# Second attention of a fused transformer block: maxima in two double PSUM slots, scores in a ring of single banks, exponentials per head

## The chip, the cores and the metric

The program runs on one core of a Trainium2 chip. The metric is the device time of one execution in microseconds; the kernel before took 1678.64 us (median of three runs, 1678.16 to 1680.62). A core has TensorE (matrix products, written PE in the profile, its weight loads PEld), VectorE (DVE), ScalarE (ACT), GpSimd (POOL) and SyncE (SP, which only issues DMAs here). Each has its own instruction stream, and they meet only at semaphores. TensorE writes to PSUM alone: eight banks, each 512 fp32 columns wide over 128 partitions. VectorE and ScalarE read PSUM; GpSimd and DMA don't.

## The reference

The block has three parts, over 4 batches of 1024 tokens of width 128: a first attention (16 heads of 64, causal), a second attention (16 heads whose keys, queries and values have 4 columns), and a mixture of 8 experts. The change lies in the second.

```
Q = (hs @ q_w + q_b).reshape(B, S, H, HD).transpose(0, 2, 1, 3)
K = (hs @ k_w + k_b).reshape(B, S, H, KPH).transpose(0, 2, 1, 3)
V = (hs @ v_w + v_b).reshape(B, S, H, KPH).transpose(0, 2, 1, 3)
scores = jnp.einsum('bhsk,bhtk->bhst', Q[..., :KPH], K) / math.sqrt(KPH)     # KPH = 4, H = 16
attn = jax.nn.softmax(scores, axis=-1)
ao = jnp.einsum('bhst,bhtv->bhsv', attn, V)
...
mla_out = ao @ o_w + o_b
```

## The kernel before, in words

**Groups and items.** The second attention is 16 groups (`N2`), number n = 4·batch + quarter; a group is 4 heads of one batch. A group has 32 items u = 0 to 31. An item's scores are those of two heads: 128 keys against 512 queries each, two matmuls of 32 contraction rows (`scores`, L1857), transposed so that keys lie on the partitions. ScalarE takes their exponentials (`exp`, L2101), and `values` (L1872) multiplies them with the values, two items later, into a PSUM bank `OT`, in four column tiles of the array (eight records an item).

**Maxima.** The exponentials need the row maxima of the scores first. So each item also has a maxima product (`maxima`, L1883): 128 queries against 512 keys for two heads, which VectorE reduces to two columns (`read_item`, L2333). They run 22 items ahead (`LEAD`), hence partly in the next group. After 16 of them the maxima of half a group are found (L1264), split into three bf16 parts by GpSimd (L2204 to L2210), turned by TensorE (`turn_tops`, L1891) and added to the query rows by VectorE (`lower_queries`, L2342), which the scores 0 or 16 of the group wait for. From item 10 of the last group on there are no maxima left; that stretch is the tail.

**PSUM.** Six banks are three double slots, given out in turn to scores and maxima (`slot(n, u, kind)`): scores(u) overwrites the slot of maxima(u-2), and waits for VectorE's read of it (`top_done`); maxima(u) overwrites the slot of scores(u-1), and waits for its exponentials (`e_done`). Bank 6 is `OT`, bank 7 is `SPARE`, which all other products share one after the other (`spare`): turned maxima, turned outputs (L1899), turned attention output (`turn_ao`, L1906), its projection (`project`, L1912), and for the next batch the turned states (L1834), queries and keys (L1840) and values (L1847). The last five come in four pieces, one an item, each between the item's maxima and its values.

**Row groups.** Heads sit on 32-row strips of the array. Scores of item u use strips 0 and 1 or 2 and 3 by u % 2; maxima m use them by m // 2 % 2. So in two items of four they are the same strips.

**Order.** There is no planner: every engine's program is written out, in the order of the functions `group`, and TensorE's order in an item is scores, maxima, spare piece, values of item u-2. Which spare piece comes at which item stands in the constants `TOPS_AT`, `OUTPUTS_AT`, `AO_AT`, `PROJECT_AT`, `HS_AT`, `QK_AT`, `LV_AT`; the items at which ScalarE copies a half of `OT` in `COPIED_AT`. Groups 1, 3 and 7 carry states and half of queries and keys of the next batch, groups 2, 6 and 10 the rest and the values, groups 4, 8 and 12 the attention output of the batch before and half its projection, groups 5, 9 and 13 the other half. Groups 11 and 14 carry none of these and are called plain here.

## Time and profile before

| | |
|---|---|
| runs | 1678.64 us median, 1678.16 to 1680.62 |
| profiled execution, first to last instruction | 1681.5 us |
| PE busy | 1618.6 us (96%) |
| DVE busy | 1440.7 us (86%) |
| ACT busy | 1208.0 us (72%) |
| POOL busy | 460.7 us (27%) |
| largest group on DVE: L2333, reads of maxima, 490 records | 585.4 us |
| largest on ACT: L2101, exponentials, 512 | 524.2 us |
| on PE: L1872 values, L1857 scores, L1883 maxima | 327.8, 198.9, 189.0 us |

The page gives no time of the profiled execution other than its span. The second attention runs from about 790 us to 1471 us of it, with maxima until 1437 us. A duration in a row is the record's own; instructions of one engine overlap at their ends, so what one costs in a stream is the distance between starts. Matmuls are recorded with their way through the array, so two that start together can each show their whole duration, and a busy TensorE need not be the bound: one looks at what each of its instructions was released by.

### The profile page before, as it was taken

Reading aid. Unit: us, or ns where it says so; the run is one execution under the profiler, and the core shown is the slowest. Engines: PE = TensorE matmul, PEld = TensorE weight load, DVE = VectorE, ACT = ScalarE, POOL = GpSimd, SP = SyncE. Lnnn points to the kernel's source line nnn. Section 1 sums busy time; section 2 is a strip of 40 time slices with the busy share of each in tenths; the row PEclk is TensorE's granted clock in tenths of the full one; section 3 lists DMA queues with packets and bytes.
Section 4 is the critical chain, followed back from the end, with each engine's and each line's share of the span. In section 5 each row is a group of like instructions: output and inputs, shape, how many; then the busy total and the mean of one; then the engine's idle time right before and its main releaser. Section 6 shows DMA issues by size and latency. Waiting matters only on the chain.

```text
span 1681.5 us, 38177 instructions
## 1 busy us (share of the span) xinstructions
PE 1618.6 (96%) x14842; PEld 712.2 (42%) x14842; DVE 1440.7 (86%) x2099; ACT 1208.0 (72%) x1208; POOL 460.7 (27%) x563
## 2 busy tenths in 40 slices
PE   7899999999999999998999999999999999989996
PEld 3444444444444444444233333333332332456774
DVE  6877777888888888996999999999999999488888
ACT  5666766666667666654887888788878888775776
POOL 4211112333332323341234232323332332220004
PEclk9999999999999999997999999999999999999998
DMA  5311111011110110011012000200030000000001
GB/s 142 72 39 37 37 37 39 20 37 37 37 37 36 37 37 21 22 32 32 14 39 51 9 12 16 48 12 13 16 74 20 13 16 21 1 8 8 14 13 50
DMA packets 46602, 52.94 MB, mean 31 GB/s; under 512 B 9279, under 2 KB 33551, under 8 KB 46482
## 3 DMA queue, kind: packets, MB, share of 16 engines
q1 hardware_dynamic: 45584, 50.05, 10.2%
q8 instruction: 84, 1.38, 0.3%
q10 hardware_dynamic: 898, 1.22, 0.3%
q14 instruction: 36, 0.29, 0.1%
HBM read 15.07 MB, written 10.49 MB: 15 GB/s over the span
## 4 chain that ended last, share of the span: by engine, by line
PE 85%; DVE 8%; ACT 3%; issue 2%; POOL 1%; ACTq 0%; POOLq 0%; DVEq 0%
PE psum L1872 15%; PE psum L590 15%; PE psum L571 11%; PE psum L1857 9%; PE psum L1883 7%; PE psum L533 5%; PE psum L1503 4%; PE psum L1470 4%; PE psum L608 3%; DVE arena L2333 3%; PE psum L628 2%; PE psum L553 1%; ACT arena L2101 1%; PE psum L554 1%; PE psum L555 1%
## 5 line engine op out<-in xcount | busy, mean ns | idle before, releaser
L2333 DVE TENSOR_REDUCE arena<-psum 128x2 f32<-128x1024 f32 x490 | 585.4, 1219 | 39.2 <-PE psum L1883 33.0
L2101 ACT ACTIVATE arena<-psum 128x1024 f32<-128x1024 f32 x512 | 524.2, 1026 | 131.6 <-PE psum L1857 117.9
L755 ACT ACTIVATE arena<-psum 128x2048 f32<-128x2048 f32 (+1 forms) x160 | 274.0, 1713 | 229.0 <-PE psum L571 228.9
L1872 PE MATMUL psum<-arena 128*32 128x256 f32 x4096 | 327.8, 392 | 0.7
L859 POOL TENSOR_SCALAR_AFFINE_SELECT arena<-arena 128x512 f32<-128x512 f32 (+1 forms) x160 | 152.5, 971 | 508.9 <-ACT arena L755 508.9
L590 PE MATMUL psum<-arena,hs 128*64 128x512 f32 (+3 forms) x1536 | 283.0, 496 | 0.2 <-POOL arena L859 0.2
L571 PE MATMUL psum<-arena 64*128 64x512 f16 (+3 forms) x2304 | 215.0, 324 | 2.1 <-DVE arena L907 1.6
L1857 PE MATMUL psum<-arena 32*128 32x512 bf16 x1024 | 198.9, 385 | 3.7 <-DVE arena L2333 3.0
L1883 PE MATMUL psum<-arena 32*128 32x512 bf16 x980 | 189.0, 382 | 6.0 <-ACT arena L2101 2.4
L907 DVE TENSOR_TENSOR arena<-arena 128x1024 f16<-128x1024 f32 x64 | 78.4, 1226 | 101.5 <-ACT arena L734 101.5
L590 PEld LDWEIGHTS psum<-arena,hs 128*64 128x64 f32 x1536 | 96.0, 136 | 141.5 <-issue 125.2
L571 PEld LDWEIGHTS psum<-arena 64*128 64x128 f16 x2304 | 96.5, 94 | 132.8 <-issue 57.1
L1857 PEld LDWEIGHTS psum<-arena 32*128 32x128 bf16 x1024 | 48.1, 91 | 215.5 <-issue 145.6
L1872 PEld LDWEIGHTS psum<-arena 128*32 128x32 f32 x4096 | 81.6, 108 | 112.1 <-issue 95.1
L1576 ACT ACTIVATE arena<-psum,b1T 128x1024 f16<-128x1024 f32 x64 | 71.3, 1115 | 51.0 <-PE psum L1470 48.3
L2204 POOL CAST arena<-arena 128x16 bf16<-128x16 f32 x32 | 8.2, 255 | 345.2 <-DVE arena L1264 345.2
L2251 POOL TENSOR_TENSOR arena<-arena,minus_one 128x16 f32<-128x16 f32 x30 | 87.2, 2906 | 53.9 <-ACT arena L2121 53.6
L1503 PE MATMUL psum<-arena 128*128 128x128 f16 x1536 | 92.6, 221 | 7.2 <-issue 5.4
L1503 PEld LDWEIGHTS psum<-arena 128*128 128x128 f16 x1536 | 89.5, 99 | 16.0 <-issue 8.7
L533 PE MATMUL psum<-arena 128*128 128x512 f16 x384 | 93.8, 381 | 0.7 <-ACT hs L740 0.4
L1349 DVE TENSOR_TENSOR arena<-arena 128x1024 f16<-128x1024 f32 x59 | 71.7, 1222 | 22.4 <-ACT arena L1577 22.2
L1470 PE MATMUL psum<-arena 128*128 128x512 f16 x384 | 88.6, 379 | 1.7 <-ACT arena L1577 1.7
(221 smaller groups left out, 2127.5 us busy)
## 6 DMA issues: line engine op xcount, KB each, us to landing
arena<-arena SPq DMA_DIRECT2D x30, 512.0 KB, 2.9
arena<-arena SPq DMA_DIRECT2D x46, 128.0 KB, 2.2
arena<-latent_q SPq DMA_DIRECT2D x64, 64.0 KB, 2.0
arena<-latent_k SPq DMA_DIRECT2D x64, 64.0 KB, 2.0
arena<-arena SPq DMA_DIRECT2D x60, 64.0 KB, 2.3
X<-in_L_attn_states SPq DMA_DIRECT2D x4, 512.0 KB, 4.6
latent_q<-arena SPq DMA_DIRECT2D x16, 96.0 KB, 2.2
latent_k<-arena SPq DMA_DIRECT2D x16, 96.0 KB, 2.3
```

The costliest lines, as they stand in the source:

```text
L533: last = nc.tensor.matmul(dst[:, half * HALF:(half + 1) * HALF], w_now[:, 2 * j + w, :], x_now[:, x, half * HALF:(half + 1) * HALF], start ...
L571: last = nc.tensor.matmul(SC[:, s, c:c + w], k[rows, kt * P:(kt + 1) * P], q[rows, q0:q0 + w], start=(m == 0), stop=(m == 2), skip_group_c ...
L590: last = nc.tensor.matmul(OUT[s * DH:(s + 1) * DH, q0:q0 + w], vals[par][:, kt, s * DH:(s + 1) * DH], probs[g][:, s, c:c + w], start=first ...
L755: nc.scalar.activation(probs[g], SC[:, :, 0:WIDTH[g]], ACT.Exp, scale=DH ** -0.5).then_inc(exp_done, 1)
L859: return nc.gpsimd.affine_select(out=v, in_=v, compare_op=ALU.is_ge, fill=0.0, base=0, pattern=[[0, blocks], [1, P]], channel_multiplier=-1)
L1470: last = nc.tensor.matmul(HP[c][:, half * HALF:(half + 1) * HALF], w1_e[par][:, w, c * P:(c + 1) * P], mT[:, x, tok], start=(m == 0), stop ...
L1503: last = nc.tensor.matmul(YP[slot][:, tok], h[slot][c][:, tok], w2_e[par][:, w, c, :], start=(c == 0 and m == 0), stop=(c == FC - 1 and m ...
L1857: last = nc.tensor.matmul(dst[:, i * HALF:(i + 1) * HALF], k_rows[par][rows, kt * P:(kt + 1) * P], q_rows[par][rows, h * HALF:(h + 1) * HA ...
L1872: last = nc.tensor.matmul(OT[ROWS * c:ROWS * (c + 1), h * HALF // 2:(h + 1) * HALF // 2], v_cols[par][:, kt, 2 * pr + i, :], e_probs[u % 4 ...
L1883: last = nc.tensor.matmul(dst[:, i * HALF:(i + 1) * HALF], q_rows[par][rows, qt * P:(qt + 1) * P], k_rows[par][rows, kh * HALF:(kh + 1) * ...
L2101: nc.scalar.activation(e_probs[u % 4], src, ACT.Exp, scale=KD ** -0.5).then_inc(e_done, 1)
L2333: nc.vector.tensor_reduce(half_tops[:, kh, qt, 2 * pr:2 * pr + 2], src.rearrange("p (i c) -> p i c", i=2), AX.X, ALU.max).then_inc(top_don ...
```

## The change

- `MAXIMA` holds two double slots (banks 0 to 3) for maxima alone: maxima(u) waits only for VectorE's read of item u-2 (`maxima_free`). In TensorE's order they now come ahead of the item's scores.
- `RING` holds three single banks (4, 5, 6). Each head's scores take one (`half_scores`), each has its own semaphore count and its own exponential over 512 columns (`half_exp`, 2 an item), and waits for the exponential three uses back (`ring_free`).
- All other products take one more bank of that ring in turn (`spares`, `ring(n, u, 2)`), each as a whole in one item: four tiles at once rather than one an item. They wait for the exponential of the item before, and the second scores item behind them waits until they were taken (`spare_taken`). Queries and keys are one matmul of 512 columns a half; values of the next batch come in two halves with a read on VectorE each. `OT` moves to bank 7.
- `maximum(n, m)` reorders maxima inside a quarter, so that their strips are always those that the item's scores don't use.
- The constants move by up to two items; the last group's tail uses the maxima slots as a double slot for scores, and exponentials of full width, as before.

`order` shows the streams as they are issued: engine instruction, tile, and the semaphores it waits for. On TensorE in group 4 around item 15, before (L1857 scores, L1883 maxima, L1872 values, L1912 projection):

```order
L1857 MATMUL psum<-arena 128x512 [waits top_done]
L1857 MATMUL psum<-arena 128x512
L1883 MATMUL psum<-arena 128x512 [waits e_done]
L1883 MATMUL psum<-arena 128x512
L1912 MATMUL psum<-arena 128x128
L1872 MATMUL psum<-arena 32x256 [waits e_done]
L1872 MATMUL psum<-arena 32x256 x3
L1857 MATMUL psum<-arena 128x512 [waits top_done,tops_ready]
L1857 MATMUL psum<-arena 128x512
L1883 MATMUL psum<-arena 128x512 [waits e_done]
L1883 MATMUL psum<-arena 128x512
L1912 MATMUL psum<-arena 128x128
```

The same place of the changed kernel (L1902 scores of a head, L1927 maxima, L1916 values, L1957 projection):

```order
L1927 MATMUL psum<-arena 128x512 [waits top_done]
L1927 MATMUL psum<-arena 128x512
L1902 MATMUL psum<-arena 128x512 [waits e_done,tops_ready]
L1902 MATMUL psum<-arena 128x512 [waits e_done]
L1957 MATMUL psum<-arena 128x128 [waits ow_in,ao_ready,e_done]
L1957 MATMUL psum<-arena 128x128 x3
L1916 MATMUL psum<-arena 32x256 [waits e_done]
L1916 MATMUL psum<-arena 32x256 x3
L1927 MATMUL psum<-arena 128x512 [waits top_done]
L1927 MATMUL psum<-arena 128x512
L1902 MATMUL psum<-arena 128x512 [waits e_done] x2
L1916 MATMUL psum<-arena 32x256 [waits e_done]
```

The maxima stand first and no longer wait for `e_done`; the two scores wait singly; the projection's four tiles stand together where one stood in each of four items, behind a wait for `e_done`.

On ScalarE around the copy of half of `OT`, before (L2101 exponential, L2115 copy, L2121 copy of turned outputs):

```order
L2101 ACTIVATE arena<-psum 128x1024 [waits ov_done,sc_done] x13
L2115 COPY arena<-psum 128x256 [waits out_turned,ov_done]
L2101 ACTIVATE arena<-psum 128x1024 [waits ov_done,sc_done] x3
L2121 COPY arena<-psum 128x256 [waits out_scaled,out_turned]
L2101 ACTIVATE arena<-psum 128x1024 [waits ov_done,sc_done] x5
```

and in the changed kernel (L2164 exponential of a head, L2184, L2190 the same copies):

```order
L2164 ACTIVATE arena<-psum 128x512 [waits sc_done]
L2164 ACTIVATE arena<-psum 128x512 [waits sc_done,ov_done]
L2184 COPY arena<-psum 128x256 [waits out_turned,ov_done]
L2164 ACTIVATE arena<-psum 128x512 [waits sc_done]
L2164 ACTIVATE arena<-psum 128x512 [waits sc_done,ov_done]
L2164 ACTIVATE arena<-psum 128x512 [waits sc_done]
L2164 ACTIVATE arena<-psum 128x512 [waits sc_done,ov_done]
L2164 ACTIVATE arena<-psum 128x512 [waits sc_done]
L2164 ACTIVATE arena<-psum 128x512 [waits sc_done,ov_done]
L2164 ACTIVATE arena<-psum 128x512 [waits sc_done]
L2190 COPY arena<-psum 128x256 [waits out_scaled,out_turned]
L2164 ACTIVATE arena<-psum 128x512 [waits sc_done,ov_done]
```

Each exponential is now two, and the copy stands between the two halves of an item.

The diff, cut to its core:

```diff
-        SLOT = [bank(0, 2), bank(2, 2), bank(4, 2)]
+        MAXIMA = [bank(0, 2), bank(2, 2)]
+        RING = [bank(4), bank(5), bank(6)]
-        OT, SPARE = bank(6), bank(7)
+        OT, SPARE = bank(7), bank(6)
-        TOPS_AT, OUTPUTS_AT = (28, 12), (20, 4)
+        TOPS_AT, OUTPUTS_AT = (29, 13), (20, 4)
-        AO_AT, PROJECT_AT, LAST_PROJECT_AT = (6, 22), 14, 27
-        HS_AT, QK_AT, LV_AT = (6, 14), (22, 6), 14
+        AO_AT, PROJECT_AT, LAST_AO_AT, LAST_PROJECT_AT = (8, 24), 16, 22, 27
+        HS_AT, QK_AT, LV_AT = (8, 16), (24, 8), (11, 16)
+        def ring(n, u, use):
+            others = sum(len(s) for s in SPARES[:n]) + sum(x < u for x in SPARES[n])
+            return RING[(2 * (ITEMS * n + u) + use + others) % 3]
+        def maximum(n, m):
+            if n == 0 and m < LEAD + 2:
+                return m // 4, m // 2 % 2, m % 2
+            return m // 4, 1 - m % 2, m // 2 % 2
...
+            def queries_keys(b, h, dst):
+                pe.wait_ge(hsT_ready, 2 * b + h + 1)
+                nc.tensor.matmul(dst, w_lat[:, :], hsT[:, h * HALF:(h + 1) * HALF], start=True, stop=True).then_inc(qk_ps, 1)
...
+            def spare(n, u):
+                kind, k, h = SPARES[n][u]
+                dst = ring(n, u, 2)
+                upto(pe, e_done, 2 * (ITEMS * n + u))
...
+            def ring_free(n, u, i):
+                at = 2 * (ITEMS * n + u)
+                if i == 0 and u - 2 in SPARES[n]:
+                    spare_taken(*SPARES[n][u - 2])
+                elif i == 0:
+                    upto(pe, e_done, at - 1 if u - 1 in SPARES[n] else at - 2)
+                else:
+                    upto(pe, e_done, at if u - 1 in SPARES[n] else at - 1)
...
                 for u in range(ITEMS):
+                    if not in_tail(n, u):
...
+                        maxima_free(n, u)
+                        maxima(n + g, (par + g) % 2, m, MAXIMA[u % 2])
                     if u % 16 == 0:
                         pe.wait_ge(tops_ready, 2 * n + u // 16 + 1)
-                        pe.wait_ge(top_done, tops_by(n + g, m))
-                    scores(par, u, slot(n, u, 0))
-                    g, m = divmod(LEAD + u, ITEMS)
-                        upto(pe, e_done, ITEMS * n + u)
-                        maxima(n + g, (par + g) % 2, m, slot(n, u, 1))
-                    spare(b, gi, u, last)
+                    if in_tail(n, u):
+                        tail_scores(n, par, u)
+                    else:
+                        for i in range(2):
+                            ring_free(n, u, i)
+                            half_scores(par, u, i, ring(n, u, i)).then_inc(sc_done, 1)
+                    if u in SPARES[n]:
+                        spare(n, u)
...
+            def half_exp(n, u, i):
+                if i == 0:
+                    upto(act, ov_done, ITEMS * n + u - 3)
+                act.wait_ge(sc_done, 2 * (ITEMS * n + u) + i + 1)
+                nc.scalar.activation(e_probs[u % 4][:, i * HALF:(i + 1) * HALF], ring(n, u, i), ACT.Exp, scale=KD ** -0.5
+                                     ).then_inc(e_done, 1)
```

## Rows read from the trace of the kernel before

**Rows 1.** Groups on VectorE, second attention while maxima run (us, mean ns | idle before).
```profile
L2333 DVE TENSOR_REDUCE arena<-psum 128x2 f32<-128x1024 f32 x490 | 585.4, 1219 | 39.2 <-PE psum L1883 33.0
```

**Rows 2.** Who waited for whom in the same stretch (us in total, times, longest).
```profile
PEld psum L1883 <- ACT arena L2101: 65.8, 221, 1.5
...
DVE arena L2333 <- PE psum L1883: 33.0, 115, 2.0
```

**Rows 3.** Timeline of all engines, quiet items (start us, us, engine).
```profile
1351.30 0.39 PE L1883 MATMUL psum<-arena 32*128 32x512 bf16 x2
...
1351.62 0.64 PE L1872 MATMUL psum<-arena 128*32 128x256 f32 x8
...
1352.19 0.39 PE L1857 MATMUL psum<-arena 32*128 32x512 bf16 x2
...
1352.41 0.39 PE L1883 MATMUL psum<-arena 32*128 32x512 bf16 x2
1352.62 2.13 ACT L2101 ACTIVATE arena<-psum 128x1024 f32<-128x1024 f32 x2 [0.27 <-PE psum L1857]
...
1353.70 0.39 PE L1883 MATMUL psum<-arena 32*128 32x512 bf16 x2
```

**Rows 4.** Timeline, VectorE: the lowering before group 0 and before group 15.
```profile
790.29 0.42 DVE L2342 TENSOR_TENSOR arena<-psum,arena 128x512 bf16<-128x512 bf16 x1 [1.77 <-PE psum L1891]
...
1423.02 0.41 DVE L2342 TENSOR_TENSOR arena<-psum,arena 128x512 bf16<-128x512 bf16 x1
```

**Rows 5.** Groups on VectorE in the plain group 11, 1259.2 to 1299.1.
```profile
L2333 DVE TENSOR_REDUCE arena<-psum 128x2 f32<-128x1024 f32 x33 | 39.1, 1220 | 1.4 <-PE psum L1883 1.1
```

**Rows 6.** Timeline, VectorE: reads with work waiting, after a lowering and a projection.
```profile
1194.70 0.41 DVE L2342 TENSOR_TENSOR arena<-psum,arena 128x512 bf16<-128x512 bf16 x1
1195.03 1.21 DVE L2333 TENSOR_REDUCE arena<-psum 128x2 f32<-128x1024 f32 x1
...
1202.28 0.68 DVE L2360 TENSOR_TENSOR acc<-psum,acc 128x512 f32<-128x512 f32 x1
1202.87 8.30 DVE L2333 TENSOR_REDUCE arena<-psum 128x2 f32<-128x1024 f32 x7
```

**Rows 7.** Timeline, TensorE: an item with a turned tile, one with a projected tile.
```profile
1100.31 0.39 PE L1857 MATMUL psum<-arena 32*128 32x512 bf16 x2
1100.31 0.39 PE L1883 MATMUL psum<-arena 32*128 32x512 bf16 x2
1100.63 0.33 PE L1834 MATMUL psum<-ident,hs 128*128 128x128 f32 x1
1100.89 0.64 PE L1872 MATMUL psum<-arena 128*32 128x256 f32 x8
...
1195.17 0.48 PE L1912 MATMUL psum<-arena 64*128 64x128 f32 x2 [0.36 <-DVE arena L2342]
1195.58 0.64 PE L1872 MATMUL psum<-arena 128*32 128x256 f32 x8
```

**Rows 8.** Timeline, ScalarE: instructions that follow each other without a wait.
```profile
847.88 0.58 ACT L2089 COPY arena<-psum 128x512 f32<-128x512 f32 x1
848.34 2.13 ACT L2101 ACTIVATE arena<-psum 128x1024 f32<-128x1024 f32 x2
...
1219.63 1.02 ACT L2101 ACTIVATE arena<-psum 128x1024 f32<-128x1024 f32 x1 [0.27 <-PE psum L1857]
1220.55 0.37 ACT L2115 COPY arena<-psum 128x256 f32<-128x256 f32 x1
```

**Rows 9.** Groups on ScalarE: the dearest half-width form.
```profile
L2095 ACT ACTIVATE arena<-psum,b_lat 128x512 f32<-128x512 f32 x6 | 4.1, 682 | 0.0
```

**Rows 10.** Windows: busy us of each engine, then the granted clock.
```profile
795.00:800.00 5.00, 4.94 (x43) 1.22 (x44) 4.74 (x9) 3.28 (x4) 0.00 (x0) 0.66 0.00 2
```

**Rows 11.** Timeline, TensorE: items at the lower clock.
```profile
796.15 0.61 PE L1857 MATMUL psum<-arena 32*128 32x512 bf16 x2
...
797.71 0.60 PE L1857 MATMUL psum<-arena 32*128 32x512 bf16 x2
```

More of the change, by code:

```diff
@@ L1848, in latent_values @@
+            def latent_values(b, h, dst):
+                pe.wait_ge(hsT_ready, 2 * b + 2)
+                for t in range(GH):
+                    at = (GH * h + t) * P
+                    last = nc.tensor.matmul(dst[:, t * LAT:(t + 1) * LAT], hsT[:, at:at + P],
                                             w_lv[:, :], start=True, stop=True, skip_group_check=True)
-                if two == GH - 1:
-                    last.then_inc(lv_ps, 1)
-            def scores(par, u, dst):
+                last.then_inc(lv_ps, 1)
@@ L1997, in turn_half @@
             def turn_half(k, h, two):
[L1999 to L2001 removed]
+                if two == 0 and k > 0:
                     pe.wait_ge(lg_ready, 2 * (k - 1) + h + 1)
```

378 lines of the change are left out of this document (196 added, 182 removed).

## Prediction, made before the changed kernel ran

> **What bounds the kernel now.** I first read the groups of instructions by line for the stretch in which maxima run (790 to 1437 us), engine by engine. TensorE is busy nearly all of it, but its records overlap, so that says little. VectorE's reads of the maxima are 490 of 1.219 us, 585 us in all, and the idle time before them is 39.2 us, nearly all put down to the maxima product [rows 1]. VectorE is therefore close to its own bound, and 39.2 us is what the trace shows it losing. The waits say why: the maxima product waited 221 times for an exponential, 65.8 us, and VectorE then waited 115 times for the maxima, 33.0 us [rows 2]. The three double slots tie the two together: maxima(u) must wait until the exponentials of item u-1 have left their slot.
>
> The timeline of two quiet items shows this loop [rows 3]. Maxima start at 1351.30, values 0.32 later, scores 0.57 after these (1352.19), maxima 0.22 after the scores (1352.41), and the next maxima at 1353.70: 2.40 us for two items. TensorE's own part of an item is thus 0.57 + 0.22 + 0.32 = 1.11 us. The rest is the wait for ScalarE: the exponential that starts at 1352.62 with 1.02 us ends at 1353.64, and the maxima go at 1353.70, 0.06 later. What VectorE needs is less: with work waiting, seven reads take 8.30 us, so (8.30 - 1.22)/6 = 1.18 us from start to start; a lowering of queries costs it 0.33 (1194.70 to 1195.03) and the addition of a projected half 0.59 (1202.28 to 1202.87) [rows 6].
>
> Fifteen groups run from the lowering at 790.29 to that at 1423.02, 632.7 us [rows 4], 42.2 a group and 1.318 an item. The plain group 11 takes 39.9 us and has only 1.4 us of idle before its reads [rows 5], so 38.5 us of it is VectorE's work (32 reads of 1.18 are 37.8, two lowerings 0.7). The gap between 39.9 and 42.2 is made in groups that carry spare pieces: each piece stands between maxima and values, and the loop through the exponentials has no room for it. One turned tile puts 0.26 us ahead of the values (1100.63 to 1100.89), one projected tile 0.41 (1195.17 to 1195.58) [rows 7].
>
> **The change, part by part.** *Maxima in their own double slot.* The wait for the exponential goes. What is late next is VectorE itself: maxima(u) is released when the read of u-2 ends. From there 0.06 to the start (as after the exponential above), 0.39 through the array, 0.04 to the read: ready 0.49 us after release, wanted 1.18 after. TensorE may be 0.69 us late without any loss.
>
> *Opposite strips.* Where maxima and scores sit on different strips, both start at 1100.31 and the next instruction comes at 1100.63 [rows 7]: 0.32 for both, against 0.22 + 0.32 on the same strips. All items but the first few now have this, so TensorE's item falls from 1.11 (or 0.90 in the half that had it) to 0.90 us. It waits 0.28 us of each 1.18 and has that to catch up with.
>
> *Exponentials per head.* ScalarE's 512-column copy costs 0.46 from start to start (847.88 to 848.34), the 1024-column exponential 0.92 (1219.63 to 1220.55) [rows 8]. Two halves are then 0.92 to 1.0; the dearest half-width form is recorded at 0.682 [rows 9]. A price below 0.46 is excluded by the columns (half of 0.92). I take 0.50 a half: 1.00 an item, 0.18 below VectorE's 1.18, and the four copies of a group fit in that. Both halves lie beside VectorE's reads and cost nothing; if that cover goes, each 0.01 us of a half above 0.57 costs 0.02 an item, some 10 us in all.
>
> *The new waits.* The second score waits for the first exponential of the item before. Scores are ready 0.49 us after their item's release, so by the prices above that exponential ends at 0.99, ahead of the next release at 1.18: no wait. A spare product waits for the second exponential of the item before, which ends at 1.49, 0.31 us into its own. Queued behind it are the values and the next maxima. With 0.4 as start, a product of X us, 0.57 of values and the 0.43 from maxima to read, VectorE goes idle only if 0.4 + X + 0.57 + 0.43 exceeds 2 x 1.18 = 2.36, that is X above 0.96 us. Turned maxima and outputs (four a group, 60 in all) are well below. Of the whole pieces that stood in four items (30: six halves each of states, queries and keys, values, attention output, projection) four turned tiles cost at most 4 x 0.26 = 1.04, four others at most 4 x 0.41 = 1.64. Upper bound: 12 x 0.08 for turns, 6 x 0.68 for queries and keys, 6 x 0.09 for projections (VectorE's own 0.59 covers the rest), none for values, 5.6 us in all; lower bound zero, since a product in one piece pays its way in and out of the array once. I take 3.
>
> The Trainium skill, TensorEngine Tiling (Array Packing), section Key Properties, says that changing the tiling mode drains the engine. By that rule most of the 0.26 of one turned tile is the switch and a fourth tile costs little, so the 3 would be nearer 0; by the row alone, times four, the turns keep their 1.04.
>
> *VectorE's other work.* Values of the next batch in two reads instead of one, three times: at most one more fixed part each, 0.5 in all. Lowerings are unchanged. The lowering for items 16 and 0 comes one item later and is done about 2.8 us after the release of item 13 or 29, with items 16 and 32 released at 3.9: no wait. SyncE's loads move only with the group's pace.
>
> *The first group.* Its start stays: the longest single wait for maxima, 2.0 us [rows 2]. Ten small ScalarE instructions stand between its exponentials; two halves and one of them are at most 1.46 us against 1.18, so 0 to 2.8, taken as 1.4. Everything else, jitter and the passage into the tail, I put at 1. The tail itself has no maxima, keeps its full exponentials and its double slot: 0, within 1 us either way.
>
> **Sum.** What stays of the idle time is 2.0 + 1.4 + 3 + 0.5 + 1 = 7.9 us. From the recorded idle: 39.2 - 7.9 = 31.3 us saved. The record leaves out gaps that are too short to count, so I also go by pace: 632.7 - 15 x 38.5 - 6 x 0.59 = 51.7 us, less three reads of values (2) and 52 small statistics instructions of groups 0 to 3, whose place in the stream no row gives (at 0.1 each, 5), is 44.7; less the lowering's own wait at 790.29, 1.8 [rows 4], and 7.9, 35.0 us. I take 34, nearer the second, since it includes what the first leaves out. The profiled span is 1681.5 us, 0.2% above the median of the runs, and the page shows nothing around it; a saving of 34 us is the same against either. 1678.6 - 34 = 1644.6 us.
>
> **Rivals.** *A: the whole pieces starve VectorE.* For: they stand in one block and wait for an exponential first. Against: the 0.28 us an item to catch up. If each of the 30 costs 0.4 us more than I took, 12 us are lost: 1657 us.
>
> *B: ScalarE sets the pace; the other side.* Place: two exponentials an item. If a half costs h from start to start, an item costs 2h plus 0.03 for the copies; the kernel is slower from 2h + 0.03 = 1.318, h = 0.645. The form at 0.682 [rows 9] would make 1.39 an item, 480 x 0.075 = 36 us lost against before: 1715 us. At 0.60, 1.23 an item, it is just under the forecast's mean item (1.318 - 34/480 = 1.247) and only leaves no room behind long pieces, about 1650. Against: the two distances of rows 8, both well below their records.
>
> *C: the lower clock; also slower.* The granted clock is 0.66 on average in 795 to 800 us, at the stage's start, behind TensorE's waits there [rows 10], and an item then takes 1.56 us (796.15 to 797.71) [rows 11], VectorE waiting. 0.66 is a mean of the two levels, 2.4 and 1.2 GHz. The changed kernel has TensorE wait in every item. It is slower from 34/(1.56 - 1.18) = 90 items at the low level; 160 make 61 us lost, 1705 us. Against: the same products in a shorter time, waits of 0.3 us at most. The Trainium skill speaks for it: TensorE: Matmul & The Clock Gate, section A second HAM failure mode: psum-queue depth-cycling, says that cycling through PSUM banks lets TensorE idle briefly so often that its clock swings. Before the change it already cycled through three slots, at full clock outside the start.
>
> *D: the change doesn't do what it says:* reads are 1.18 apart only in short runs, and 1.20 is the real pace. Then 480 x 0.02 = 10 us less: 1655.
>
> **Chances.** Forecast 0.62, with its own range 1635 to 1652; A 0.14; D 0.10; B 0.05, of which 0.03 slower and 0.02 no change; C 0.05; something unforeseen in the waits 0.04, of which 0.03 slower. The range takes in A, D and B at 0.60: 1634 (nearly all of the 44.7 gone) to 1666. A change of 0.2%, 3.4 us, is about what a measurement of this kernel can tell from none. Faster: 0.62 + 0.14 + 0.10 = 0.86; the same 0.02 + 0.01 = 0.03; slower 0.03 + 0.05 + 0.03 = 0.11.
>
> **What would show it.** VectorE's idle before reads below 10 us, with no wait of the maxima product for ScalarE; reads 1.18 apart in quiet items; a plain group of 38.5 to 39 us and the other groups from 4 on within 1.5 us of it; exponentials of 512 columns recorded near 0.59 with under 1.1 us for a pair from start to start; the clock at 1.00 through the stage. It would be wrong if exponential pairs fill ScalarE, if TensorE's waits name the exponentials ahead of scores in quiet items, or if the items behind a whole piece run well over 1.18 us.

## The result, and the profile after

The changed kernel takes 1631.11 us (median of 4 runs, 1628.53 to 1633.24) against 1678.46 (4 runs, 1678.16 to 1680.62) for the kernel before on the same chip: a ratio of 0.9703, 95% interval 0.9685 to 0.9722. The forecast of 1644.6 had the direction and what the change frees, but the gain is 47 us, not 34, and 1631.1 lies 3 us below its range: the forecast priced VectorE's read of the maxima at 1.18 us where it costs 1.131.

The profiled executions differ by 50.1 us (1681.5 against 1631.4). VectorE's lowerings ahead of group 0 and of group 15 say where:

```profile
786.19 0.42 DVE L2417 TENSOR_TENSOR arena<-psum,arena 128x512 bf16<-128x512 bf16 x1 [0.49 <-PE psum L1936]
...
1370.44 0.41 DVE L2417 TENSOR_TENSOR arena<-psum,arena 128x512 bf16<-128x512 bf16 x1
```

The fifteen groups take 584.3 us, against 632.7 [rows 4]: 48.5 saved. The 4.1 us ahead of group 0 and the 2.6 lost behind group 15 (258.4 us to the end before, 261.0 now) go with the clock, as shown below.

The groups on VectorE and ScalarE over the whole program (busy us, mean ns | idle before):

```profile
L2408 DVE TENSOR_REDUCE arena<-psum 128x2 f32<-128x1024 f32 x490 | 565.7, 1214 | 11.1 <-PE psum L1927 9.8
L2164 ACT ACTIVATE arena<-psum 128x512 f32<-128x512 f32 x980 | 519.6, 600 | 52.0 <-PE psum L1902 46.1
```

The idle time before the reads fell from 39.2 [rows 1] to 11.1. That is 28 us of 48.5: the rest is in the busy time, which fell by 20 although nothing about the read changed. A group's busy time counts records that overlap once, so reads that follow each other closely look cheaper. The waits, from 786 to 1383 us:

```profile
PEld psum L1927 <- DVE arena L2408: 190.5, 391, 1.1
...
PEld psum L1902 <- ACT arena L2164: 16.3, 73, 0.9
...
PEld psum L1944 <- ACT arena L2164: 12.0, 30, 0.4
```

The maxima product now waits for VectorE, 391 times, and hardly for the exponential any more (22 waits, 3.6 us in all, against 221 and 65.8 [rows 2]). The second row is the new wait of the scores for a bank of the ring, small. The third is the wait of one kind of spare use, the turned outputs, for the second exponential of the item before: 0.40 each, as forecast. In the chain that ended last VectorE has now 22% and ScalarE 10% (8% and 3% before).

A run of reads in the plain stretch after the lowering at 1179.30, and the reads of plain group 11, which answer to [rows 6] and [rows 5]:

```profile
1179.30 0.41 DVE L2417 TENSOR_TENSOR arena<-psum,arena 128x512 bf16<-128x512 bf16 x1
1179.63 12.53 DVE L2408 TENSOR_REDUCE arena<-psum 128x2 f32<-128x1024 f32 x11
```

```profile
L2408 DVE TENSOR_REDUCE arena<-psum 128x2 f32<-128x1024 f32 x33 | 37.8, 1215 | 0.0
```

Eleven reads in 12.53 us with a record of 1.22 are (12.53 - 1.22)/10 = 1.131 us from start to start. This is the number that the forecast had at 1.18. It is no new pace: in the kernel before, the first four reads behind the lowering at 1259.19 stand (4.61 - 1.21)/3 = 1.133 apart (first row, the view ending at 1263.5). The seven reads from which the forecast took 1.18 hold 0.1 us of idle time between them (second row, by groups from 1202.9 to 1211), which the timeline does not print, since it joins reads across gaps as short as these:

```profile
1259.52 4.61 DVE L2333 TENSOR_REDUCE arena<-psum 128x2 f32<-128x1024 f32 x4
...
L2333 DVE TENSOR_REDUCE arena<-psum 128x2 f32<-128x1024 f32 x7 | 8.2, 1217 | 0.1
```

In the changed kernel, group 11 lasts 37.3 us instead of 39.9: 32 x 1.131 = 36.2, two lowerings of 0.33, two findings of maxima of some 0.2. With no idle time left it is VectorE's own work.

ScalarE's halves (the first five of a run of seven, with the view ending at 1185.4; the whole run; one that had to wait) and TensorE's items where it catches up behind a spare use:

```profile
1183.42 2.56 ACT L2164 ACTIVATE arena<-psum 128x512 f32<-128x512 f32 x5
...
1183.42 3.64 ACT L2164 ACTIVATE arena<-psum 128x512 f32<-128x512 f32 x7
...
1187.50 0.60 ACT L2164 ACTIVATE arena<-psum 128x512 f32<-128x512 f32 x1 [0.17 <-PE psum L1902]
```

```profile
1186.97 0.39 PE L1927 MATMUL psum<-arena 32*128 32x512 bf16 x2
1186.98 0.52 PE L1902 MATMUL psum<-arena 32*128 32x512 bf16 x2
1187.43 0.64 PE L1916 MATMUL psum<-arena 128*32 128x256 f32 x8
1188.00 0.39 PE L1927 MATMUL psum<-arena 32*128 32x512 bf16 x2
1188.01 0.53 PE L1902 MATMUL psum<-arena 32*128 32x512 bf16 x2
1188.46 0.64 PE L1916 MATMUL psum<-arena 128*32 128x256 f32 x8
1189.03 0.39 PE L1927 MATMUL psum<-arena 32*128 32x512 bf16 x2
```

Seven halves take 3.64 us, (3.64 - 0.60)/6 = 0.507 each. But this run, too, hides a wait: its first five take 2.56 with a last record of 0.64, so (2.56 - 0.64)/4 = 0.48 each, and no two in the second attention are closer. The price of a half is 0.48, a pair 0.96 (0.50 and 1.00 forecast). TensorE's items are 1.03 us here (1186.97, 1188.00, 1189.03), not 0.90. The records of the two scores say why: 0.39 where both start together, but 0.52 and 0.53 here, so the second starts 0.14 late, at 1188.15. It waits for the first exponential of the item before, which runs from 1187.50 to 1188.10. Where nothing waits, the item is the 0.90 of the forecast:

```profile
1096.20 0.39 PE L1927 MATMUL psum<-arena 32*128 32x512 bf16 x2
1096.20 0.39 PE L1902 MATMUL psum<-arena 32*128 32x512 bf16 x2
1096.52 0.64 PE L1916 MATMUL psum<-arena 128*32 128x256 f32 x8
...
1097.09 0.39 PE L1927 MATMUL psum<-arena 32*128 32x512 bf16 x2
```

Two items thus make a loop: 0.52 from a score to the start of its exponential (1186.98 to 1187.50), 0.60 of exponential, 0.05 to the second score of the next item, 0.31 to its values, 0.57 to the next maxima and scores: 2.05, or 1.03 an item. That is below VectorE's 1.131, so it does not set the pace, but it limits how fast the others catch up.

The clock over five stretches (busy us of each engine, then granted clock, DMA share, GB/s):

```profile
772.00:776.00 4.00, 3.93 (x36) 2.30 (x36) 2.28 (x5) 0.88 (x1) 0.00 (x0) 0.58 0.00 0
776.00:1370.00 594.00, 561.53 (x6138) 193.85 (x6138) 579.53 (x627) 539.24 (x1049) 195.03 (x256) 1.00 0.11 29
1370.00:1411.00 41.00, 40.31 (x414) 17.29 (x411) 24.06 (x35) 33.10 (x47) 10.45 (x11) 1.00 0.01 2
1411.00:1421.20 10.20, 10.20 (x67) 4.52 (x60) 2.53 (x8) 3.32 (x4) 1.03 (x1) 0.50 0.01 2
1421.20:1631.00 209.80, 185.63 (x1996) 133.48 (x1992) 175.32 (x521) 148.42 (x163) 29.21 (x24) 0.96 0.06 19
```

It stays at its upper level, 2.4 GHz, through all groups, although TensorE waits in nearly every item. It drops to the lower level, 1.2 GHz, for 10.2 us in the tail and for 3.4 more from 1448.5, and to 0.58 on average ahead of group 0. Neither belongs to the change: group 0 began between 785.4 and 792.8 us in the traces of the twelve variants below, and at 792.6 in a second trace of the changed kernel. That is why the experiments are read by the length of the fifteen groups, which was 584.3 and 584.8 in two traces of the same kernel, beside the ratio.

The groups are not wholly free of it. The kernel before stood at the lower level for a long stretch ahead of group 0 and for another inside it (first two rows), and b_whole, below, has one in group 2 (third row):

```profile
777.90:791.60 13.70, 13.70 (x61) 8.74 (x60) 6.12 (x20) 5.01 (x5) 1.32 (x6) 0.50 0.34 77
795.00:798.40 3.40, 3.40 (x26) 0.72 (x24) 3.27 (x5) 1.71 (x3) 0.00 (x0) 0.50 0.00 0
...
894.10:897.50 3.40, 3.40 (x32) 0.72 (x24) 1.75 (x2) 1.71 (x2) 1.01 (x1) 0.50 0.77 168
```

Group 0 lasts 42.7 us before, but 41.6 in b_whole, which leaves that group as it is and runs it at the upper level. So about 1 of the 48.5 us is the clock's.

### The profile page after: what moved, and what is told of

Its sections match the earlier page's. It is cut to its first block, busy times and chain, and to the rows that moved or that the text cites. A ratio compares the mean times of both kernels' runs of the same rounds, so it can differ in the third digit from the quotient of the medians.

```text
span 1631.4 us, 38607 instructions
## 1 busy us (share of the span) xinstructions
PE 1551.1 (95%) x14806; PEld 701.8 (43%) x14806; DVE 1419.4 (87%) x2102; ACT 1227.8 (75%) x1698; POOL 461.1 (28%) x563
## 3 DMA queue, kind: packets, MB, share of 16 engines
q10 hardware_dynamic: 898, 1.22, 0.3%
## 4 chain that ended last, share of the span: by engine, by line
PE 63%; DVE 22%; ACT 10%; issue 3%; POOL 1%; ACTq 0%; POOLq 0%; DVEq 0%
DVE arena L2408 16%; PE psum L590 15%; PE psum L571 12%; ACT arena L2164 7%; PE psum L1916 5%; PE psum L533 5%; PE psum L1547 5%; PE psum L1514 4%; PE psum L608 3%; PE psum L1927 3%; PE psum L628 3%; PE psum L1902 1%; PE psum L553 1%; PE psum L554 1%; PE psum L555 1%
## 5 line engine op out<-in xcount | busy, mean ns | idle before, releaser
L2408 DVE TENSOR_REDUCE arena<-psum 128x2 f32<-128x1024 f32 x490 | 565.7, 1214 | 11.1 <-PE psum L1927 9.8
L2164 ACT ACTIVATE arena<-psum 128x512 f32<-128x512 f32 x980 | 519.6, 600 | 52.0 <-PE psum L1902 46.1
L1916 PE MATMUL psum<-arena 128*32 128x256 f32 x4096 | 329.2, 393 | 1.4 <-ACT arena L2184 0.2
L1902 PE MATMUL psum<-arena 32*128 32x512 bf16 x1024 | 255.9, 385 | 1.3 <-ACT arena L2164 0.4
L1927 PE MATMUL psum<-arena 32*128 32x512 bf16 x980 | 189.9, 384 | 21.0 <-DVE arena L2408 13.1
L1927 PEld LDWEIGHTS psum<-arena 32*128 32x128 bf16 x980 | 46.1, 91 | 231.9 <-DVE arena L2408 190.5
L1916 PEld LDWEIGHTS psum<-arena 128*32 128x32 f32 x4096 | 82.0, 108 | 113.1 <-issue 95.3
L1902 PEld LDWEIGHTS psum<-arena 32*128 32x128 bf16 x1024 | 79.0, 90 | 38.8 <-ACT arena L2164 16.3
L533 PE MATMUL psum<-arena 128*128 128x512 f16 x384 | 93.8, 381 | 0.7 <-ACT hs L740 0.4
```

What stands on the lines that cost most here:

```text
L533: last = nc.tensor.matmul(dst[:, half * HALF:(half + 1) * HALF], w_now[:, 2 * j + w, :], x_now[:, x, half * HALF:(half + 1) * HALF], start ...
L1902: return nc.tensor.matmul(dst, k_rows[par][rows, kt * P:(kt + 1) * P], q_rows[par][rows, h * HALF:(h + 1) * HALF], start=True, stop=True)
L1916: last = nc.tensor.matmul(OT[ROWS * c:ROWS * (c + 1), h * HALF // 2:(h + 1) * HALF // 2], v_cols[par][:, kt, 2 * pr + i, :], e_probs[u % 4 ...
L1927: last = nc.tensor.matmul(dst[:, i * HALF:(i + 1) * HALF], q_rows[par][rows, qt * P:(qt + 1) * P], k_rows[par][rows, kh * HALF:(kh + 1) * ...
L2164: nc.scalar.activation(e_probs[u % 4][:, i * HALF:(i + 1) * HALF], ring(n, u, i), ACT.Exp, scale=KD ** -0.5).then_inc(e_done, 1)
L2408: nc.vector.tensor_reduce(half_tops[:, kh, qt, 2 * pr:2 * pr + 2], src.rearrange("p (i c) -> p i c", i=2), AX.X, ALU.max).then_inc(top_don ...
```

## Experiments

Each ratio is to the kernel before, run on the same chip, with its 95% interval. "Groups" is the length of the fifteen groups in the trace: 632.7 us before, 584.3 after; "plain" is group 11: 39.9 and 37.3.

### Whose pace was it before: shorter reads and split reads

b_short and a_short reduce 384 of 512 columns of each maximum, in the kernel before and in the changed one.

```diff
-  src.rearrange("p (i c) -> p i c", i=2),
+  src.rearrange("p (i c) -> p i c", i=2)[:, :, 0:384],
```

> Kernel before, with VectorE's reads of the maxima over 384 instead of 512 columns of each head (a quarter of the keys is left out of the maximum), 0.27 us less a read at one column a cycle. Theory L: the loop through the exponentials stays; scores wait a little less for the read; under 20 us faster, plain groups still above 38 us. Theory V: plain groups fall by up to 0.1 us or more an item until the loop binds, so over 40 us faster.

b_short: 0.9971 (0.9957 to 0.9985), groups 625.2, plain 39.9, as before. Of the 7.5 us that the groups gain, 3.5 lie in group 0, some of it the clock's. A quarter less to read gives nothing in the plain group. So the kernel before was not at VectorE's bound even there; the idle time appears at once in the waits:

```profile
DVE arena L2333 <- PE psum L1883: 130.5, 329, 1.3
PEld psum L1883 <- ACT arena L2101: 68.6, 227, 1.5
```

VectorE waits 130.5 us instead of 33.0 [rows 2], and the maxima product waits for the exponential as long as it did.

> Changed kernel, with the same shorter reads (384 of 512 columns of each head, a quarter of the keys left out of the maximum). Both theories have VectorE as the bound here. It falls until ScalarE binds at two exponentials of 0.507 us and a share of copies, 1.04 to 1.06 an item, against 1.13 plus lowerings (37.3 us a plain group): a plain group of 33.5 to 34.5 us, 40 to 50 us faster than the changed kernel. If instead the changed kernel is already bound by ScalarE or TensorE, under 15 us.

a_short: 0.9641 (0.9618 to 0.9664), groups 567.5, plain 36.0: faster by 17 us in the groups and by 10 in the whole, where 40 to 50 were expected. VectorE could go at 0.96 or less, but the loop of 1.03 us an item described above takes over, and in quiet items the maxima products come 1.03 apart:

```profile
1335.35 0.39 PE L1927 MATMUL psum<-arena 32*128 32x512 bf16 x2
...
1336.38 0.39 PE L1927 MATMUL psum<-arena 32*128 32x512 bf16 x2
```

ScalarE, which the expectation had as the next bound, is not it: a pair of its halves costs 0.96. The waits of the maxima product for VectorE fall from 190.5 to 35.2 us. VectorE is thus the changed kernel's bound by a narrow margin: below it lies the loop, at 1.03 against 1.131.

b_split_reads and a_split_reads read the same columns in two instructions instead of one, which adds a fixed part to VectorE's item and nothing else.

```diff
-  nc.vector.tensor_reduce(half_tops[..., 2 * pr:2 * pr + 2], src..., AX.X, ALU.max).then_inc(top_done, 1)
+  for i in range(2):
+      last = nc.vector.tensor_reduce(half_tops[..., 2 * pr + i:2 * pr + i + 1], src[:, i * HALF:(i + 1) * HALF]..., AX.X, ALU.max)
+  last.then_inc(top_done, 1)
```

> The kernel before with the same split of each read into two. Theory P (the kernel before is paced by the loop through the exponentials at 1.25 an item even in its plain group, where a read costs 1.131; so 0.1 us of VectorE's time an item is free there): the plain group rises by 0 to 1 us, and the whole by under 15 us, since the maxima's slot comes free 0.06 to 0.1 us later only where that is the last wait. Rival R (the price of the read in this kernel was 1.18 to 1.20, as forecast, and its plain group is VectorE's own time): the plain group rises by 32 x 0.06 to 0.1 = 1.9 to 3.2 us and the whole by 25 to 45 us.

> The changed kernel with each read of maxima (two results, 1024 columns) issued as two reads of one result and 512 columns each, signalled once at the end: VectorE gets one more fixed part an item. From the reads of 384 columns instead of 512, start to start 0.86 to 0.96 at least against 1.131, the fixed part is 0.06 to 0.1 us. Theory P (the read costs 1.131 from start to start, and VectorE sets the pace in all quiet items of the changed kernel): the quiet reads go to 1.19 to 1.23 and the plain group from 37.3 to 39.2 to 40.5; 480 x 0.06 to 0.1 less what the pieces' stalls give back: 20 to 45 us slower than the changed kernel, 1651 to 1676. Rival T (TensorE's item, 1.03 us at least, with its waits sets the pace too): under 12 us slower.

b_split_reads: 1.0015 (1.0001 to 1.0029), groups 634.9, plain 39.9. a_split_reads: 0.9849 (0.9829 to 0.9868), groups 605.0, plain 39.4. A run of halves in a_split_reads:

```profile
1252.24 0.41 DVE L2420 TENSOR_TENSOR arena<-psum,arena 128x512 bf16<-128x512 bf16 x1
1252.57 9.65 DVE L2409 TENSOR_REDUCE arena<-psum 128x1 f32<-128x512 f32 x16
```

A half costs (9.65 - 0.68)/15 = 0.598 us, a pair 1.196, so the split adds 0.065 an item. In the changed kernel the plain group pays all of it (32 x 0.065 = 2.1, measured 2.1), and the groups 20.7 of 31. The rest comes out of the stalls behind spare uses: counted as under *Whole pieces* below, they fall from 13.0 to about 3 us. In the kernel before, the plain group pays nothing: its 1.247 us an item had room for a read of 1.196. This settles the price of the read (1.131) and refutes the forecast's reading of the plain group as VectorE's work. The scores' waits for a read of two items back could have made VectorE part of the pace all the same (first row, before, from 790 to 1437 us); b_split_reads nearly doubles them (second row, the same stretch) and the plain group does not move, so other waits cover them:

```profile
PEld psum L1857 <- DVE arena L2333: 66.4, 151, 1.0
...
PEld psum L1857 <- DVE arena L2334: 125.3, 284, 1.1
```

### The loop through the exponentials

b_half_exps keeps everything of the kernel before but issues each exponential as two.

```diff
-  nc.scalar.activation(e_probs[u % 4], src, ACT.Exp, ...).then_inc(e_done, 1)
+  for i in range(2):
+      now = slice(i * HALF, (i + 1) * HALF)
+      last = nc.scalar.activation(e_probs[u % 4][:, now], src[:, now], ACT.Exp, ...)
+  last.then_inc(e_done, 1)
```

> The kernel before, with each exponential of 1024 columns issued as two of 512 in the same double slot, signalled once at the end of the second. ScalarE's pair then takes 1.014 us instead of 0.92 from start to start. Theory L (the loop maxima - values - scores - exponential sets the pace of the kernel before): each item whose maxima wait for the exponential gets 0.09 us longer, 480 x 0.07 to 0.09 = 34 to 43 us slower, less where other things hide it: 20 to 43 us, ratio 1.012 to 1.026; the plain group goes from 39.9 to 42 to 43 us. Rival V (VectorE's read sets the pace at 1.18 to 1.20 in the plain group): the plain group stays below 41 us, and the whole is under 15 us slower.

1.006 (1.0039 to 1.0082), groups 645.1, plain 40.9. That is 12.4 us in the groups and some 10 in the whole: both below the range of theory L, and both within what rival V allowed. By this run alone V would stand; it is b_short and b_split_reads that exclude it. What I had wrong is the size, twice over. The loop passes one exponential in two items ([rows 3]: maxima at 1351.30 and 1353.70; the maxima product waited 221 times [rows 2], not 480), and who waits for a pair pays 1.08 instead of 1.02, which is 0.06 more and not 0.09:

```profile
1353.28 1.08 ACT L2103 ACTIVATE arena<-psum 128x512 f32<-128x512 f32 x2 [0.27 <-PE psum L1857]
1354.42 0.39 PE L1883 MATMUL psum<-arena 32*128 32x512 bf16 x2
...
1356.88 0.39 PE L1883 MATMUL psum<-arena 32*128 32x512 bf16 x2
...
PEld psum L1883 <- ACT arena L2103: 78.7, 230, 1.5
```

Two items take 2.46 us here and 2.40 before. At 0.06 in two items the plain group should lose 16 x 0.06 = 1.0, which it does, and the fifteen groups 14; they lose 12.4, and the wait grew by 12.9 from 65.8.

b_own_slots gives the maxima two double slots in the kernel before, and leaves one, with whole exponentials, to the scores.

```diff
-  return SLOT[(2 * ITEMS * n + 2 * u + kind) % 3]
+  return SLOT[u % 2] if kind else SLOT[2]
...
+  else:
+      upto(pe, e_done, ITEMS * n + u)
   scores(par, u, slot(n, u, 0))
```

> The kernel before, with the maxima in two double slots of their own, and the scores in the one double slot that is left, with whole exponentials. The maxima no longer wait for ScalarE, but the scores of an item wait for the exponential of the item before. Worked out: scores start 0.06 after the exponential's end, 0.43 to the first number that the next exponential can read, exponential 0.96: a loop of about 1.43 us an item against 1.32 now, 480 x 0.11 = 50 us slower, between 30 and 70 (ratio 1.018 to 1.042), and the plain group goes from 39.9 to 45 us or more. This tells whether the ring of single banks and the exponentials by half are needed for the gain, or whether it comes from the maxima's own slots alone: by that rival this kernel is 20 us or more faster than before.

1.0648 (1.0615 to 1.0681), groups 737.8, plain 48.5. It is slower by twice what I worked out: 48.5/32 = 1.52 us an item instead of 1.43. (Group 10 takes 53.8 where its like take 49; 13.6 us of it are at the lower clock.) The timeline shows the loop bare:

```profile
1500.98 0.39 PE L1857 MATMUL psum<-arena 32*128 32x512 bf16 x2 [0.34 <-ACT arena L2104]
...
1501.41 1.02 ACT L2104 ACTIVATE arena<-psum 128x1024 f32<-128x1024 f32 x1 [0.49 <-PE psum L1857]
1502.58 0.39 PE L1857 MATMUL psum<-arena 32*128 32x512 bf16 x2 [0.63 <-ACT arena L2104]
```

0.43 from scores to exponential, 1.02 of exponential, then 0.06 (0.15 here) to the scores: 1.51. I had put the exponential at 0.96, near its distance from start to start, and added up to 1.43 what makes 1.45; who waits for it sees the whole record. So the maxima's own slots alone lose 105 us in the groups, some 5 of them by the clock, and halves alone 12; the two together with the ring of single banks gain.

### Strips

b_strips puts the opposite strips into the kernel before, a_old_strips takes them out of the changed one.

In b_strips:

```diff
+        def maximum(n, m):
...
+            return m // 4, 1 - m % 2, m // 2 % 2
...
-                qt, pr, kh = m // 4, m // 2 % 2, m % 2
+                qt, pr, kh = maximum(n, m)
```

In a_old_strips:

```diff
-            return m // 4, 1 - m % 2, m // 2 % 2
+            return m // 4, m // 2 % 2, m % 2
```

> Kernel before, with only the order of the maxima changed (maximum(n, m)), so that maxima and scores of an item always sit on different strips of the array. Theory L (the kernel before was paced by the loop scores, exponentials, maxima, and a read costs VectorE only 1.13 us from start to start): TensorE's part falls by 0.2 us in half of the items, but the maxima still wait for the exponentials; a part of it comes back where TensorE ended the wait last: 0 to 15 us faster. Theory V (the kernel before was paced by VectorE at 1.18 a read in quiet items): 0 to 5 us faster. Theory S (opposite strips are most of the gain of the change): 30 us or more faster.

> Changed kernel with the old order of maxima, so that in half of the items maxima and scores share strips of the array. TensorE's part of such an item is 1.11 instead of 0.90 us, still below VectorE's 1.13. Theory L: quiet items unchanged, less room behind spare products: 2 to 10 us slower than the changed kernel. Theory S (opposite strips carry the gain): 25 us or more slower.

b_strips: 1.0000 (0.9978 to 1.0023), groups 626.5, plain 39.9: 6.3 us gained in the groups, none of it in the plain one, and none to be seen in the whole time, whose runs spread from 1672.7 to 1687.6. About 1 of the 6.3 is the clock's, in group 0. a_old_strips: 0.9779 (0.9748 to 0.9811), groups 595.5, plain 37.4: 11.3 us lost in the groups, 0.1 of it in the plain one. So the strips are worth 5 to 11 us of the 48.5, as room for TensorE behind spare uses. The rest comes with the slots, the ring and the halves together; b_half_exps and b_own_slots show that neither halves nor slots alone give it, and no run takes it apart further.

### Whole pieces

b_whole issues the spare pieces of the kernel before whole, in one item each.

```diff
-  turn_states(begun, 0, piece(u, HS_AT[0]))
+  whole(lambda t: turn_states(begun, 0, t), u, HS_AT[0])
```

> The kernel before, with its spare pieces (turned maxima outputs, turned states, queries and keys, projections, latent values) issued whole in one item, as the changed kernel does, and nothing else of the change. Theory L (the kernel before is paced by the loop through the exponentials, and a piece pays its way in and out of the array once): four parts in four items lengthen four loops by 0.26 to 0.41 us each, one whole piece lengthens one loop by less than their sum, so the fifteen groups (632.7 us) lose 5 to 15 us: ratio 0.991 to 0.997. Rival W (whole pieces starve VectorE, which has no more than one item ahead): each of some 90 whole pieces costs more than its four parts: 5 to 20 us slower.

1.003 (1.0011 to 1.005), groups 633.8: neither theory. Groups 6 and 10 lose 0.4 us each. Group 2 loses 1.3, but holds 3.4 us at the lower clock, and group 0 gains 1.1, since the low stretch of the kernel before is absent. The others stay within 0.1. One whole piece costs that loop about what its four parts do.

In the changed kernel, the distance between two reads less 1.131 and less what other instructions lie between (record less 0.09; a finding of maxima counted as 0.2) is the stall. The stalls sum to 13.0 us: 3.5 behind item 8, 0.9 behind 11, 1.5 behind 16, 2.7 behind the turned outputs at 20, 3.3 behind 24, 1.1 in group 0. The longest, queries and keys in group 7:

```profile
1093.94 0.39 PE L1927 MATMUL psum<-arena 32*128 32x512 bf16 x2
1093.94 0.53 PE L1902 MATMUL psum<-arena 32*128 32x512 bf16 x2
1094.57 1.13 PE L1887 MATMUL psum<-arena,w_lat 128*128 128x512 f32 x2
1095.62 0.64 PE L1916 MATMUL psum<-arena 128*32 128x256 f32 x8
...
1096.20 0.39 PE L1927 MATMUL psum<-arena 32*128 32x512 bf16 x2
```

The product comes 0.63 behind the scores instead of 0.45, holds the values back by 1.05, and the read that waits for the maxima at 1096.20 comes late; VectorE is recorded idle for 0.73 us. a_moved puts four pieces into items that follow a longer VectorE instruction; a_again is the changed kernel itself beside it.

```diff
-        AO_AT, PROJECT_AT, LAST_AO_AT, LAST_PROJECT_AT = (8, 24), 16, 22, 27
-        HS_AT, QK_AT, LV_AT = (8, 16), (24, 8), (11, 16)
+        AO_AT, PROJECT_AT, LAST_AO_AT, LAST_PROJECT_AT = (8, 18), 16, 22, 27
+        HS_AT, QK_AT, LV_AT = (8, 24), (15, 8), (11, 15)
```

> The changed kernel with four of its whole pieces in other items: attention output of the second half in item 18 instead of 24, turned states of the second half in 24 instead of 16, queries and keys of the first half in 15 instead of 24, latent values of the second half in 15 instead of 16; all work is done. In the changed kernel's trace the read behind such a piece comes 0.2 to 0.8 us late, and least where VectorE has just done something else (the lowering, the addition of a projected half). If those stalls are real losses on the path (theory: VectorE sets the pace, and only gaps between its reads cost time), a piece two items behind such an instruction costs less: 3 to 5 us faster than the changed kernel on the same chip. Rival: the stalls are made up for later by TensorE and ScalarE and cost nothing: within 1 us.

> The changed kernel itself once more, beside the others on the same chip, as their base: 1628 to 1634 us.

a_moved: 0.9733 (0.9713 to 0.9754), groups 586.7; a_again: 0.9702 (0.9678 to 0.9726), 1633.05 us, groups 584.8. The move lost 2 us in the groups instead of gaining 3 to 5: queries and keys at 15 still stall the next read by 0.44, turned states at 24 by up to 0.35 in their place, latent values at 15 by 0.63 where it was 0.49, and attention output at 18 by 0.74 where it was 0.38. The rule for the places was wrong; what makes item 18 worse stays open.

a_spares_late leaves the places and issues a spare use's product behind the values of its item, so that they run while it would wait; a_scalar_spares_late does so for three kinds.

```diff
+  late = u in SPARES[n] and SPARES[n][u][0] in ("ao", "states", "queries_keys", "outputs", "project", "latent_values")
-  if u in SPARES[n]:
+  if u in SPARES[n] and not late:
       spare(n, u)
...
   values(n - 1, 1 - par, ITEMS + u - 2)
+  if late:
+      spare(n, u)
```

> The changed kernel with TensorE's part of every extra use of the ring but the turned maxima (turned outputs, turned attention output, projections, turned states, queries and keys, latent values) issued behind the values of its item instead of ahead of them. In the changed kernel such a product waits about 0.4 us for the second exponential of the item before, with the values queued behind it; here the values run in that time. The stalls of VectorE behind these uses sum to about 12 us in the changed kernel's trace (0.17 to 0.82 each). Theory E (each stall is the exponential's wait plus the product's own length): the stalls fall by 0.3 to 0.4 each where they are that long, 15 groups from 584.3 to 574 to 579: 5 to 10 us faster than the changed kernel. Rival X (the stall is the product's own length and its reader on ScalarE or VectorE, which now comes later): 15 groups stay within 2 us of 584.3 or get longer.

> The same for attention output, states and queries and keys alone, which stand in front of ScalarE's reader and make the longest stalls (0.24 to 0.82 us, some 7 to 8 us in all). Theory E: 15 groups 2 to 5 us shorter than 584.3. Rival X: within 1 us, or longer.

a_spares_late: 1628.79 us (1627.18 to 1629.21), 0.9675 (0.9659 to 0.9690), groups 579.7, stalls 8.0. a_scalar_spares_late: 1626.93 us (1626.20 to 1633.60), 0.9676 (0.9654 to 0.9698), groups 581.8. The groups are 4.5 and 2.5 us shorter than in the changed kernel; plain groups stay at 37.3. Theory E holds in part: the stalls behind items 8, 20 and 24 fall from some 9.5 to 4.3 us, those behind 11 and 16 hardly, and the groups gain 4.5 us (2.5 in the second kernel, within its 2 to 5), where 5 to 10 were expected. So a stall is in part the wait of 0.4. The ratios' intervals overlap with the changed kernel's, so only the groups show the step; by them, a_spares_late is the fastest kernel that does all the work.

## Why the prediction was right, and where not

- **The bound.** Right that TensorE and ScalarE wait on each other through the shared slots and that freeing the maxima of them makes VectorE the bound: a_split_reads pays for a longer read in every plain item. Wrong that the kernel before was at VectorE's bound in its plain group: b_short and b_split_reads leave that group at 39.9.
- **The read at 1.18: the failed step.** It came from "8.30 us for seven" [rows 6]. Records of 1.22 at a distance of 1.131 overlap by 0.09, so a wait of up to 0.09 behind each read leaves no gap between records, and the timeline joins reads across short gaps besides. Seven reads at 1.131 take 6 x 1.131 + 1.22 = 8.01, so the run held 0.3 us of waits, 0.1 of them recorded as idle, and was no run "with work waiting". The price is 1.131. Over fifteen plain-size groups that is 15 x (38.5 - 37.3) = 18 us more room. The forecast's second way then gives 35.0 + 18 = 53, less 5.1 for stalls of 13.0 instead of 7.9: 47.9, measured 48.5, or 47.4 without the clock's 1. That it comes so close is partly luck, since the 7.9 holds terms that are no stalls behind pieces (2.0 for the start, 1 for the rest). The first way, by recorded idle time, could not see it either.
- **"No wait" for the second score.** I let the first exponential end 0.99 us after its item's release, from 0.43 to its start and 0.50 for its length. It is 0.06 + 0.52 + 0.60 = 1.18, just behind the next release at 1.131. In quiet items that is hidden; behind a long piece it stretches TensorE's item from 0.90 to 1.03 and leaves 0.10 us an item to catch up, not 0.28.
- **Whole pieces at 3 us.** The stalls outside group 0 are 11.9, 2.7 of them behind turned outputs, which the forecast put "well below". With a read of 1.131 and the same terms, the piece that VectorE can hide is 2 x 1.131 - 0.4 - 0.57 - 0.43 = 0.86 us, and queries and keys take 1.05. The lengths of the pieces were safe bounds: four turned tiles of states stand 0.58 us ahead of the values, not 4 x 0.26 = 1.04,

```profile
919.43 0.66 PE L1881 MATMUL psum<-ident,hs 128*128 128x128 f32 x4
920.01 0.64 PE L1916 MATMUL psum<-arena 128*32 128x256 f32 x8
```

  and turned attention output 0.53 (958.75 to 959.28). By the Trainium skill's rule on the drain (TensorEngine Tiling (Array Packing), section Key Properties) the 3 would have been nearer 0. These tiles agree with the rule, a fourth one being cheap, though no run measured the drain by itself; the stalls did not fall with it. Even turned states stall a read by 0.2, where the formula gives none, so the formula lacks a term. TensorE's being still late from the piece before is an argument for it that no run tested.
- **ScalarE's halves** at 0.50 from start to start (0.48 at the least), the spare use's wait at 0.4, the first group at 1.4 (1.1): right. The tail, from the lowering ahead of group 15 to the end, at equal 3.4 us of lower clock: 258.4 and 258.5 us in kernels with the old slots (before, b_whole), 256.8 and 257.6 with the new ones (a_spares_late, a_split_reads), so 0.8 to 1.7 shorter, at the edge of the 1 us that was forecast or past it.
- **Rivals.** A: the mechanism is real, but costs 9 us behind the 30 pieces rather than 15, and 3 behind the turned outputs. B is refuted by 0.48 a half. C is refuted: 1.00 through the groups, with TensorE waiting 391 times for VectorE. The Trainium skill's rule (TensorE: Matmul & The Clock Gate, section A second HAM failure mode: psum-queue depth-cycling) did not show in this kernel. D is refuted in the other direction: the pace is below 1.18.
- **The signs.** VectorE's idle time before the reads is 11.1, just above the 10 named; the plain group is 37.3, below 38.5 to 39; groups 6 and 10 are 2.5 us longer than it, not 1.5 at most. Reads behind whole pieces come up to 0.82 us late, which the forecast had named as a sign of being wrong.
- **Chances.** The range's low end came from "nearly all of the 44.7 gone"; 44.7 itself carried the price of the read, which I held for exact, since the timeline printed no gap in the run that it was read from. That price had needed bounds too.

## What to carry to other kernels

An engine's own pace is the smallest distance between two starts, not the mean over a run that looks unbroken: overlapping records hide waits as long as their overlap, and a view that joins records hides more. The same care is due on the next engine: the 0.507 of ScalarE's seven halves looked just as unbroken, and the price is 0.48. Who waits for an instruction pays its whole record and the way to its start instead; use the first price for an engine's work and the second for a loop. Before calling a stage bound by an engine, make that engine's instruction a little longer or shorter: where the stage does not move, it is a loop.

## What the runs showed of the hardware that was not expected

- A reduction on VectorE of 1024 fp32 PSUM columns costs 1.131 us from start to start with a record of 1.22; two of 512 cost 0.598 each with a record of 0.68. The second instruction adds 0.065. The Trainium skill (Perfetto Trace Analysis, section Optimizing Scalar/DVE Operations) gives about 125 ns of access overhead for VectorE on PSUM, and says that a record is longer than the engine's own time because part of it lies under the next instruction. The second half of that is what these reads show (1.22 against 1.131); what one more instruction adds here, 0.065, is half of the page's figure.
- An exponential on ScalarE of 512 fp32 PSUM columns costs 0.48 us from start to start when it need not wait, with a record of 0.60 to 0.64; two of them in one wait cost 1.08 where one of 1024 columns costs 1.02.
- From a score product to its exponential's start it is 0.43 us where maxima follow on the same strips ([rows 3], 1352.19 to 1352.62), and 0.52 where maxima and scores run on all four strips at once (1186.98 to 1187.50).
- TensorE's clock was at its lower level in the tail for 3 to 17 us in all, in one or two stretches between 1384 and 1521, at other places in each execution of both kernels (b_own_slots, whose tail comes later, left out here). The time from the lowering ahead of group 15 to the end follows: 256.8 to 258.5 us with 3.4 or 6.8 us of it, 260.6 to 263.0 with 13.6 or 17. The start of group 0 moves by up to 7 us in the same way: 785.4 to 786.3 us with 3.4 us of lower clock ahead of it, 790.3 to 790.9 with 17, 792.2 to 792.8 with 20.5.
